# A four-layer graph network on one Trainium2 core: the first feed-forward product of layer 0 by halves of the nodes, degree rows by DMA, W1 fetched during attention, Wo with four outputs open

## The reference

```
layer 0:  z = ln(h);  h += attention(z) @ Wo + bo        # 8 heads, over the edges, with an edge bias
          z = ln(h);  ff = silu(z @ W1 + b1) @ W2 + b2   # 512 -> 1024 -> 512
          result = h + ff
layer 1:  mean over the incoming edges (divided by max(count, 1)), two 512x512 products, batch norm, relu
layer 2:  two graph convolutions 512 -> 1024 -> 512, scaled on both sides by 1/sqrt(degree + 1)
layer 3:  sum over the edges, two 512x512 products, layer norm
```

## Time and profile before

| | us |
|---|---|
| median of 3 runs | 388.41 (388.33 to 388.44) |
| the profiled execution | 388.6 |
| its span, first to last instruction | 387.1 |
| TensorE busy | 367.4 (95%) |
| VectorE busy | 312.8 (81%) |
| ScalarE busy | 170.9 (44%) |

### The profile page before, as it was taken

How to read it: one execution, slowest core, us unless ns; L and a number is a source line. 1 busy time by engine, 2 the same in 40 slices (tenths; PEclk the granted TensorE clock), 3 DMA queues, 4 the chain that set the end, 5 groups by cost and what they waited for, 6 DMA issues and landing times.

```text
span 387.1 us, 5100 instructions
## 1 busy us (share of the span) xinstructions
PE 367.4 (95%) x1782; PEld 280.8 (73%) x1782; DVE 312.8 (81%) x660; ACT 170.9 (44%) x287; POOL 4.2 (1%) x19
## 2 busy tenths in 40 slices
PE   2879999999999999999999999999999999999994
PEld 1545566676667898997678788887588878787883
DVE  5889999999939899987858976598875778488356
ACT  4754765464126432525559433262364521135320
POOL 4000000000000000000000000000000000000000
PEclk9999999999999999999999999999999999999999
DMA  6602445343217000159200512300500032000002
GB/s 235 262 1 70 134 160 159 109 136 107 80 36 263 3 3 0 46 174 352 81 2 1 179 39 94 124 0 0 187 32 0 3 125 92 3 0 0 2 11 98
DMA packets 16360, 32.92 MB, mean 85 GB/s; under 512 B 1360, under 2 KB 1488, under 8 KB 16336
## 3 DMA queue, kind: packets, MB, share of 16 engines
q1 hardware_dynamic: 15744, 32.25, 24.0%
q10 hardware_dynamic: 592, 0.36, 0.3%
HBM read 21.07 MB, written 1.05 MB: 57 GB/s over the span
## 4 chain that ended last, share of the span: by engine, by line
PE 78%; DVE 14%; ACT 4%; issue 2%; DMA 1%; DVEq 0%; ACTq 0%
PE acc L1397 12%; PE bank L1379 11%; PE bank L1482 7%; PE bank L1272 6%; PE bank L1273 6%; PE bank L1253 4%; PE acc L1253 4%; PE acc L1272 4%; PE acc L1273 4%; PE bank L1467 4%; PE acc L1453 3%; DVE big_rounded L651 2%; PE acc L1230 2%; PE bank L1230 2%; PE acc L1550 2%
## 5 line engine op out<-in xcount | busy, mean ns | idle before, releaser
L1397 PE MATMUL acc<-wide_rounded,c_rounded 128*126 128x512 f32 x200 | 59.5, 439 | 0.7 <-ACT acc L463 0.7
L1397 PEld LDWEIGHTS acc<-wide_rounded,c_rounded 128*126 128x126 f32 x200 | 37.0, 187 | 19.7 <-issue 13.0
L791 DVE TENSOR_SCALAR wide_rounded<-iota_f,picked 128x512 fp32r<-128x512 f32 x100 | 42.2, 480 | 1.5 <-issue 1.1
L482 ACT COPY z_sb<-acc 126x512 f32<-126x512 f32 x37 | 21.6, 585 | 41.9 <-PE acc L1397 33.1
L624 DVE TENSOR_TENSOR wslot_rounded<-wslot,wide_rounded 128x512 fp32r<-128x512 f32 x24 | 16.2, 688 | 21.3 <-ACT wslot L376 21.3
L506 ACT ACTIVATE wide<-wide,low_col 128x512 f32<-128x512 f32 x32 | 20.5, 713 | 25.4 <-DVE low_col L904 25.3
L1482 PEld LDWEIGHTS bank<-v_sb,big 128*128 128x128 f32 x256 | 29.7, 192 | 2.2 <-issue 2.2
L1482 PE MATMUL bank<-v_sb,big 128*128 128x65 f32 x256 | 30.9, 275 | 0.0
L797 DVE TENSOR_TENSOR c_rounded<-row_bc,wslot_rounded 128x1008 fp32r<-128x1008 bf16 x25 | 30.0, 1200 | 0.0
L1379 PE MATMUL bank<-t_sb,wslot 128*128 128x512 f32 x64 | 29.5, 594 | 0.5 <-ACT t_sb L458 0.5
L651 DVE TENSOR_TENSOR big_rounded<-big,big_rounded 128x1024 fp32r<-128x1024 f32 x24 | 29.1, 1222 | 0.5
(11 more groups left out here) (310 smaller groups left out, 763.5 us busy)
## 6 DMA issues: line engine op xcount, KB each, us to landing
big<-z_sb SPq DMA_DIRECT2D x36, 252.0 KB
big<-in_w SPq DMA_DIRECT2D x4, 2048.0 KB, 7.7
x_sb<-in_x SPq DMA_DIRECT2D x8, 256.0 KB, 4.7
big<-in_w_3t SPq DMA_DIRECT2D x2, 1024.0 KB, 6.8
row_bc<-in_rows SPq DMA_DIRECT2D x7, 256.0 KB, 6.3
wslot<-in_wq SPq DMA_DIRECT2D x1, 1024.0 KB, 9.0
wslot<-in_wk SPq DMA_DIRECT2D x1, 1024.0 KB, 10.9
wslot<-in_wv SPq DMA_DIRECT2D x1, 1024.0 KB, 12.9
```

The costliest lines, as they stand in the source:

```text
L482: nc.scalar.copy(stage[0:BROWS, b % STAGES, :], a).then_inc(S["staged"], 1)
L791: nc.vector.tensor_scalar(hot_ring[:, u, k, :], iota_f[:, :], picked[:, 0, s0 + k:s0 + k + 1], None, ALU.is_equal)
L1397: last = nc.tensor.matmul(to, st_ring[:, u, 2 * k + a, :, :].rearrange("p w k -> p (w k)"), hot_ring[:, u, k, :], start=False, stop=False, ...
```

## The change

Four edits, all in layer 0:

- **Wo**: `product_in_parts` is called with `group=NT, by_tile=NT`: the highs of all four outputs are issued piece by piece, and the low terms follow output by output. On VectorE the sum, the moments, the coefficients and the plain step of neighbouring tiles are interleaved anew; ScalarE makes the plain step of tiles 0 and 1 (`z_plain`), VectorE that of tiles 2 and 3.
- **ff1 by halves of the nodes**: z is turned into banks by halves (`z_turned_at`): banks 0 and 1 hold the left 256 nodes, two feature tiles in each, banks 2 and 3 the right ones. ScalarE evacuates pieces of 256 columns (`half_turned`), 16 of them instead of 8 of 512. The highs of the first four outputs are issued by halves, 32 products of 256 columns instead of 16 of 512; the other four outputs and all low terms stay at 512.
- **Degree rows by DMA**: the matrices on the diagonal, the two products and the two copies go. SyncE, after asking for W2, sends each of the two degree columns (128 x 4) into one row of partition 0, waits, spreads this row to 128 partitions, and waits again. `rcnt_ready` and `dinv_ready` are now waited for where the rows are first used.
- **W1 fetched during attention**: into memory that Wk and Wv have left (`w1_raw`), once the products for q, k and v are done. Its first rounding on ScalarE precedes that of the attention output and waits for the end of attention, since the rounded W1 takes the place of attention tables.

The core of the diff (waits that follow from it and removed helpers are left out):

```diff
+            sp.wait_ge(S["qkv_mm"], 3 * NT)
+            sp.dma_start(w1_raw.rearrange("p (k a) n -> p k (a n)", a=2), k_major(w1_0)).then_inc(S["w1_0_in"], 16)
             sp.wait_ge(S["st_mm"], UNITS)
...
-            load("w1_0", w1_0)
             load("w2_0", w2_0)
+            for name, column, spread in (("rcnt", rcnt_c, rcnt_bc), ("dinv", dinv_c, dinv_bc)):
+                sp.wait_ge(S[name + "_column"], 1)
+                for t in range(NT):
+                    sp.dma_start(deg_row[0:1, t * P:(t + 1) * P], column[:, t:t + 1]).then_inc(S[name + "_row"], 16)
+                sp.wait_ge(S[name + "_row"], 16 * NT)
+                sp.dma_start(spread, deg_row.unsqueeze(1).broadcast_to([1, P, N])).then_inc(S[name + "_ready"], 16)
+                sp.wait_ge(S[name + "_ready"], 16)
             sp.wait_ge(S["ff1_mm"], FT)
             load("w_lr", wl_t, 0)
...  ScalarE
+            act.wait_ge(S["pv_mm"], 2 * NT)
+            weight_hi("w1_0", 0)
             for t in range(NT):
                 act.wait_ge(S["turned"], NT + t + 1)
                 hi_part("att", t, t_at, bank[t][:, :])
...
+            def half_turned(half, k, to, done):
+                if k % 2 == 0:
+                    act.wait_ge(S["turned"], 2 * NT + 2 * half + k // 2 + 1)
+                nc.scalar.activation(to[:, k, half * N // 2:(half + 1) * N // 2], z_turned_at(half, k), ACT.Identity,
+                                     bias=colp("ln2_b", k), scale=colp("ln2_g", k)).then_inc(S[done], 1)
+            ln_std(2, 0)
+            z_plain(0)
+            ln_std(2, 1)
+            z_plain(1)
+            ln_std(2, 2)
+            for k in range(NT // 2):
+                half_turned(0, k, t_at.rounded, "ff_half")
+            ln_std(2, 3)
+            for k in range(NT // 2, NT):
+                half_turned(0, k, t_at.rounded, "ff_half")
+            half_turned(0, 0, t_lo.full, "t_ready")
+            for k in range(NT):
+                half_turned(1, k, t_at.rounded, parts["ff_in"][0])
+            for k in range(1, NT):
+                half_turned(0, k, t_lo.full, "t_ready")
+            for k in range(NT):
+                half_turned(1, k, t_lo.full, "t_ready")
...  VectorE
+            weight_lo("w1_0", 0, 1)
+            weight_lo("w1_0", 1, 2)
+            for t in range(NT):
+                dve.wait_ge(S["wo_mm"], t + 1)
+                nc.vector.tensor_tensor(h_sb[:, t, :], bank[4 + t][:, :], h_sb[:, t, :], ALU.add
+                                        ).then_inc(S["wo_added"], 1)
+                if t >= 1:
+                    ln_coef(2, t - 1)
+                dve.wait_ge(S["wo_added"], t + 1)
+                moments(t, h_sb, "ln_var")
+            ln_plain(2, 2, h_sb)
+            ln_coef(2, 3)
+            ln_plain(2, 3, h_sb)
...  TensorE
-            product_in_parts(hi, halves(t_at, c1_lo), halves(c1_hi, t_lo), reads("att"), "wo_mm", group=2)
+            product_in_parts(hi, halves(t_at, c1_lo), halves(c1_hi, t_lo), reads("att"), "wo_mm", group=NT,
+                             by_tile=NT)
+            for t in range(2):
+                pe.wait_ge(S["z_scalar"], 2 + t + 1)
+                turn_z(t)
+            for k in range(NT - 1):
+                half_highs(0, k)
+            pe.wait_ge(S["z_ready"], 3)
+            turn_z(2)
+            half_highs(0, NT - 1)
+            pe.wait_ge(S["z_ready"], 4)
+            turn_z(3)
+            for k in range(NT):
+                half_highs(1, k)
+            for m in range(NT, FT):
+                pe.wait_ge(S["t_ready"], NT + 2 * (m - NT) + 2)
+                for k in range(NT):
+                    nc.tensor.matmul(bank[FF1_BANKS[m]][:, :], tile(w1[k][0], m), t_at.rounded[:, k, :],
+                                     start=(k == 0), stop=False)
```

More of the change, by code:

```diff
@@ L269, in blocks_out, with z_turned_at @@
             return 16 * sum(len(block_parts(i)) for i in range(k, b, STAGES))
+        def z_turned_at(half, k):
+            return bank[2 * half + k // 2][:, k % 2 * N // 2:(k % 2 + 1) * N // 2]
         block = ctx.enter_context(nc.Block())
@@ L398, in weight_hi @@
                 lo, hi = weights[name]
[L399 to L408, removed]
+                whole = w1_raw if name == "w1_0" else lo.full
+                nc.scalar.copy(hi.rounded[:, part, :], whole[:, part, :]).then_inc(S[name + "_hi"], 1)
             act.wait_ge(S["eps_column"], 1)
@@ L518, in _, with z_plain @@
                 hi_part("att", t, t_at, bank[t][:, :])
-            act.wait_ge(S["deg_parts"], NT)
             nc.scalar.activation(dinv_c[:, :], deg[:, :], ACT.Sqrt, bias=1.0).then_inc(S["deg_std"], 1)
[L521 to L531, removed]
+            for q in range(1, 4):
+                weight_hi("w1_0", q)
+            def z_plain(t):
+                act.wait_ge(S["ln_coef"], 2 * NT + t + 1)
+                nc.scalar.activation(z_sb[:, t, :], h_sb[:, t, :], ACT.Identity, bias=shift[:, t:t + 1],
+                                     scale=rstd[:, t:t + 1]).then_inc(S["z_scalar"], 1)
+            def half_turned(half, k, to, done):
[20 more added lines that the diff above has]
+                half_turned(1, k, t_lo.full, "t_ready")
             for f in range(FT):
@@ L649, in weight_lo @@
                 lo, hi = weights[name]
+                whole = w1_raw if name == "w1_0" else lo.full
                 dve.wait_ge(S[name + "_hi"], after)
[L651 removed]
+                nc.vector.tensor_tensor(lo.rounded[:, part, :], whole[:, part, :], hi.rounded[:, part, :].bitcast(F32),
                                         ALU.subtract).then_inc(S[name + "_lo"], 1)
@@ L1200, in turn @@
                     last.then_inc(S[done], 1)
[L1202 to L1211, removed]
             def halves(hi, lo, n=NT):
@@ L1237, in product_by_row, with product_in_parts @@
                     last.then_inc(S[done], 1)
-            def product_in_parts(banks, lhs, rhs, ready, done, group=1, weight_lo=None, second=None, started=False,
-                                 by_tile=0, free={}):
+            def product_in_parts(banks, lhs, rhs, ready, done, group=1, weight_lo=None, started=False,
+                                 by_tile=0):
                 terms = list(zip(lhs, rhs))
                 def highs(m):
-                    if second and m == NT:
-                        pe.wait_ge(*second)
                     for k, (a, r) in enumerate(terms):
@@ L1537, in _, with turn_z @@
-            product_in_parts(FF1_BANKS, weight("w1_0", NT), halves(t_at, t_lo), reads("ff_in"), "ff1_mm",
-                             group=FT, weight_lo="w1_0_lo", second=(S["t_ready"], 2 * NT), by_tile=NT,
-                             free={2: (S["rcnt_ready"], 1), 3: (S["dinv_ready"], 1)})
+            product_in_parts(hi, halves(t_at, c1_lo), halves(c1_hi, t_lo), reads("att"), "wo_mm", group=NT,
+                             by_tile=NT)
+            def turn_z(t):
+                half, at = t // 2, t % 2 * P
+                for k in range(NT):
+                    last = nc.tensor.transpose(z_turned_at(half, k)[:, at:at + P], tile(z_sb[:, t, :], k), ident[:, :])
+                    if t % 2 == 1 and k % 2 == 1:
+                        last.then_inc(S["turned"], 1)
@@ new lines, in _, with half_highs @@
+            w1 = weight("w1_0", NT)
+            def half_highs(half, k):
+                nodes = slice(half * N // 2, (half + 1) * N // 2)
+                pe.wait_ge(*((S["ff_half"], k + 1) if half == 0 else reads("ff_in")[k][0]))
+                for m in range(NT):
+                    if half == k == 0:
+                        pe.wait_ge(S["wo_added"], FF1_BANKS[m] - NT + 1)
+                    nc.tensor.matmul(bank[FF1_BANKS[m]][:, nodes], tile(w1[k][0], m), t_at.rounded[:, k, nodes],
+                                     start=(half == k == 0), stop=False)
@@ new lines, in _ @@
+            pe.wait_ge(S["w1_0_lo"], 4)
+            for m in range(FT):
+                to = bank[FF1_BANKS[m]][:, :]
+                for k in range(NT):
+                    if m == 0:
+                        pe.wait_ge(*reads("ff_in")[k][1])
+                    nc.tensor.matmul(to, tile(w1[k][0], m), t_lo.rounded[:, k, :], start=False, stop=False)
+                    last = nc.tensor.matmul(to, tile(w1[k][1], m), t_at.rounded[:, k, :], start=False,
+                                            stop=(k == NT - 1))
+                last.then_inc(S["ff1_mm"], 1)
```

45 lines of the change are left out of this document (17 added, 28 removed).

## The result

The changed kernel takes 385.20 us (median of 6 runs, 384.90 to 385.52) against 388.41 (6 runs, 388.33 to 388.44): a ratio of 0.9917 [0.9907, 0.9927], 3.2 us less. The profiled execution of the changed kernel took 385.18 (span 383.4), before 388.6 (387.1): 3.42 less. The spans differ by 0.3 more, because before, SyncE's last instruction ends the span 0.3 behind TensorE's, and after it does not. From the start on, its times run 0.09 earlier (Wo starts at 175.69, before at 175.78).

The account below looks back on a forecast made before the run. TensorE, 78% of the chain, bounds the kernel where it waits between Wo and ff1's low terms. Terms -0.27, +0.77 and -2.79 sum to -2.29: 388.6 becomes 386.3, median 386.1, range 385.3 to 388.4 for 8 in 10.

Parts of the forecast that it names:

- Wo with four outputs open: Wo product on TensorE: only the first wait stays, end 186.97 against 187.81; of 0.84 us, 0.27 is left.
- VectorE becomes the pace: Layer norm after Wo: VectorE needs 2.01 us a tile against outputs every 1.84; last plain step at 190.89.
- ff1 by halves: From last plain step to right half +0.77 us, from there to ff1's low terms -2.79; first low product 198.64.
- both unknown prices: In ff1, a 256-column product on TensorE taken at 0.123 us, a 256-column evacuation on ScalarE at 0.45.
- Rivals 1 and 2: ff1: half products no cheaper than whole ones, 388.7, chance 0.12; ScalarE's half pieces cost 0.67 each, 388.4, chance 0.08.
- W1 early: W1's load and first rounding, ending at 174.71 before the first turned piece at 175.04: nothing gained by itself.
- gain nothing: Degree products and copies taken off TensorE and VectorE lay beside waits: no gain, at most 0.05 us.
- The sync queue: Degree rows behind W2: spreads 2.0 to 6.3 us, queue free at about 200, before the next weights: cost nothing.
- high ends: Sync queue's highest prices: small transfers 6.8 us, spread 6.3; first spread issued at 188.2, queue free at 210.6.
- Rival 3: Sync queue still spreading degree rows when next weights are due; from 218.8 each microsecond costs one: 395 us, chance 0.10.

Follow-up runs that it names:

- e1: The changed kernel with VectorE made to wait for the end of each layer-norm step before the next: 385.83 us.
- e2: The changed kernel with the Wo product as before (two outputs ahead instead of four), all else as changed: 385.87 us.
- e6: The kernel before with W1 fetched during attention, its rounding where it was, nothing else changed: 388.37 us.
- e3: The kernel before with Wo's four outputs open and nothing else changed: 388.62 us.
- e5: The kernel before with the degree rows spread by DMA and nothing else changed: 388.37 us.
- e7: The changed kernel with the second degree column's spread sent once more, with its own wait: 385.16 us.
- e9: The changed kernel with the second degree column's spread sent twice more, each with its own wait: 397.64 us.

## Why the prediction came out as it did

The mechanism held: the gain is made between Wo and ff1's low terms and carried to the end. The size did not. Between the two profiled executions 3.42 us went, where 2.29 were forecast: 3.00 on the walk, 0.33 later on, 0.09 ahead of Wo.

- **Wo with four outputs open: right in its first half.** Last product started at 186.55, 186.6 foreseen.
- **"VectorE becomes the pace", 2.01 us a tile: this step failed.** Measured 1.84, TensorE's pace. I had added 0.72, 0.93 and 0.36 as rows 4 show them, each with the wait behind it. In the new order most neighbours have none, and overlap. The last plain step ended at 190.07, not 190.89. With the 0.09 at the start taken off it moved by 1.00 instead of 0.27 (191.16 - 190.07 - 0.09), and that is the missing 0.7: the 0.77 of Wo's earlier end was kept whole, and the way from there grew shorter too. The chain itself doesn't pass through this plain step but through the moments of tile 3. They ended at 188.76, 189.37 foreseen, 0.6 earlier; the rest came from shorter steps around ScalarE (0.61 from the start of a half piece to its product, 191.51 to 192.12, where I took 0.45 + 0.25). With the waits put back, e1's moments end at 189.39 and its end is 0.63 later: there the forecast's price holds. The hint stood in the earlier trace rows: there the reciprocal starts 0.10 after an aggregation of 0.18.
 The Trainium skill, VectorE: DVE Perf Modes, section The DRAIN you can't avoid, has it, from a row of eight copies, that a semaphore between neighbours costs nothing extra. Here it cost 0.11 in each of two places of a tile, and e1 is 0.6 us slower; the measurement decides.
- **ff1 by halves: both unknown prices right.** Half products 0.124 apart (192.12 to 194.11 for sixteen; 0.123 taken), half pieces 0.458 (0.45 taken). Rivals 1 and 2 are out. From the last plain step to the right half's first product it took 2.05 (2.11 foreseen), from there to the low terms 5.72 (5.64). TensorE met no wait at the banks. Before, these two stretches took 1.34 and 8.43: the 2.0 that e2 leaves to the halves.
- **W1 early: right**, nothing by itself (e6), and no delay of Wo.
- **Degree rows: "gain nothing" was off by 0.3.** In layer 1's batch norm the kernel before has a late reciprocal; the square root it waits for had ended at 272.24. First the timeline of VectorE before, then after:

```profile
272.20 0.15 DVE L1059 TENSOR_SCALAR bn_mean<-bn_mean 128x1 f32<-128x1 f32 x1
272.70 0.16 DVE L1061 RECIPROCAL rstd<-std 128x1 f32<-128x1 f32 x1 [0.35 <-DVE bn_mean L1059]
```

```profile
269.12 0.15 DVE L1085 TENSOR_SCALAR bn_mean<-bn_mean 128x1 f32<-128x1 f32 x1
269.31 0.16 DVE L1087 RECIPROCAL rstd<-std 128x1 f32<-128x1 f32 x1
```

 It is 0.50 from start to start in the one, 0.19 in the other: 0.31 of the 0.33. The kernel before, e3 and e6 have this stop; all kernels with the degree rows by DMA, e5 among them, don't. So it goes with that edit, which shortens VectorE's list; why the stop is there was not tried and stays open. In e5's profiled execution it offsets 0.31 of the 0.53 by which the walk is longer; the five quicker runs of e5 fit a gain of this size.
- **The sync queue: right in its outcome, wrong in a price.** A spread took 11.2 us, beyond my 2.0 to 6.3; only because the small transfers were through sooner than at my high ends was the queue free at 209.7, inside my 187 to 210.6. The first spread was issued at 183.39 and not at 188.2, and 3.9 us instead of 8.8 lay between its landing and the second one's issue. That these errors cancelled is luck. By the Trainium skill, SBUF — State Buffer, section Door 1: The DMA port swizzle, a spread was estimated at 9.6, 1.6 less than from issue to landing, and the trace agrees with its 27 GB/s: that is what moved in 194 to 196 of e5's table, with the DMA engines 87% busy. Rival 3's point was wrong too (e7, e9): it lies near 221.4, since TensorE needs the late tile later than VectorE needs the weight.

The medians differ by 3.2 and not 3.4 because the execution profiled before lies 0.2 above its median.

## What to carry to other kernels

When an order of steps changes, don't price the new order from durations that carry the old order's waits: take the distance from start to start of neighbours that stand in the same relation, with or without a wait between them. An edit that is worth nothing alone may be the half of a pair (Wo's open outputs and VectorE's new order), so try edits in company as well as alone; and a median that doesn't move may hide a gain and a loss, so look at its single runs and their clocks (e5). And put whatever releases another engine, here a turn, ahead of products that are ready but that nobody waits for.

## What the runs showed of the hardware

- VectorE steps without a wait between them overlap by about 0.1 us each (the kernel after against e1): a step of 0.69 is followed after 0.61 instead of 0.72, one of 0.16 after 0.08 instead of 0.19.
- A spread of 2 KB from one partition to 128 took 11.2 us from issue to landing in every kernel that has it, while a row of the same size from memory took 6.5 (median of seven, kernel after).
- TensorE's granted clock was 0.50, the lower level, behind a wait of 1.68 us (e5's profiled execution) and behind one of 7.69 us (e9); in the place of the first, the kernel after has products and shows 1.00 from 184 to 202 us.
